# Running sums of a three-layer graph network: VectorE's loop written out, ScalarE waiting on the count of sums

## What is computed

```
def _gcn_layer(x, src, dst, norm, W, b, n_nodes):
    h = x @ W
    msg = h[src] * norm[:, None]
    out = jax.ops.segment_sum(msg, dst, num_segments=n_nodes)
    return out + b
```

## Time and profile before

| what | value |
|---|---|
| median of 3 runs (lowest, highest) | 11817.82 us (11795.35, 11846.04) |
| the profiled execution | 11829.28 us, of which the profile's span is 11827.6 us |
| busy time PE, DVE, ACT, POOL | 2554.4, 3860.8, 1826.5, 5887.5 us |
| SCALAR_TENSOR_TENSOR of the sums (line 896) | 4689, 2311.4 us busy, 493 ns each |
| indirect DMAs of the laps (line 824) | 4608, 4356.3 us busy, 945 ns each |

### The profile page before, as it was taken

How to read it: one execution, slowest core, us unless ns; L and a number is a source line. 1 busy time by engine, 2 the same in 40 slices (tenths; PEclk the granted TensorE clock), 3 DMA queues, 4 the chain that set the end, 5 groups by cost and what they waited for, 6 DMA issues and landing times. The chain is left out here.

```text
span 11827.6 us, 59944 instructions
## 1 busy us (share of the span) xinstructions
PE 2554.4 (22%) x11366; PEld 2079.0 (18%) x11366; DVE 3860.8 (33%) x7516; ACT 1826.5 (15%) x2792; POOL 5887.5 (50%) x6228
## 2 busy tenths in 40 slices
PE   6090000000040000000030000000262766655570
PEld 5070000000030000000030000000151655444460
DVE  7574333333332333333333333333340111100127
ACT  0000111111131111111131111111110111111120
POOL 0003666666636666666646666666437233344411
PEclk9999999999985555555565555555665877777785
DMA  0005555555554555555555555555441111111127
GB/s 15 9 0 162 180 180 191 179 180 186 177 168 158 182 186 180 176 183 176 180 161 174 183 183 177 182 175 191 157 140 24 36 37 37 34 34 34 34 85 223
DMA packets 586804, 1580.96 MB, mean 134 GB/s; under 512 B 134656, under 2 KB 373580, under 8 KB 547948
## 3 DMA queue, kind: packets, MB, share of 16 engines
q1 hardware_dynamic: 306828, 897.27, 21.2%
q0 software_dynamic: 278608, 668.34, 19.2%
q10 hardware_dynamic: 1296, 14.68, 0.3%
HBM read 820.05 MB, written 759.77 MB: 134 GB/s over the span
## 5 line engine op out<-in xcount | busy, mean ns | idle before, releaser
L824 POOL DMA_INDIRECT acc<-feature_table,staged_indices x4608 | 4356.3, 945 | 3043.4 <-issue 1523.7
L896 DVE SCALAR_TENSOR_TENSOR ps<-ps,keep_within_node,acc 128x256 f32<-128x256 f32 x4689 | 2311.4, 493 | 4521.2 <-issue 3756.1
L1205 POOL DMA_INDIRECT acc<-attention_table,idx x1024 | 972.6, 950 | 1312.5 <-DVEq L1422 978.1
L862 PE MATMUL ps<-work,carry_from_partition 128*128 128x256 f32 x6 | 3.7, 713 | 6986.2 <-ACT work L777 6986.2
L862 PEld LDWEIGHTS ps<-work,carry_from_partition 128*128 128x128 f32 x6 | 1.5, 309 | 6987.2 <-ACT work L777 6987.2
L777 ACT COPY acc<-ps 128x1024 f32<-128x1024 f32 x594 | 601.1, 1012 | 3249.0 <-remote 1664.4
L777 ACT COPY work<-ps 128x1024 f32<-128x1024 f32 x579 | 585.3, 1011 | 2370.9 <-remote 1006.0
L1284 PE MATMUL ps<-work 128*128 128x256 f32 x3136 | 801.8, 402 | 524.8 <-issue 451.1
L1294 PE MATMUL ps<-work,onehot 128*128 128x256 f32 x3136 | 783.2, 394 | 544.5 <-issue 501.1
L1384 DVE TENSOR_TENSOR acc<-ps,work 128x512 f32<-128x512 f32 x196 | 135.4, 691 | 2329.6 <-DMA feature_table<-acc 1057.0
L1284 PEld LDWEIGHTS ps<-work 128*128 128x128 f32 x3136 | 630.9, 202 | 681.2 <-issue 522.3
(11 more groups left out here) (308 smaller groups left out, 2226.4 us busy)
## 6 DMA issues: line engine op xcount, KB each, us to landing
unning_features_of_edges<-acc SPq DMA_DIRECT2D x147, 2048.0 KB
unning_features_of_edges<-work SPq DMA_DIRECT2D x144, 2048.0 KB
acc<-feature_table,staged_indices POOLq DMA_INDIRECT x4608
expert_rows<-acc SPq DMA_DIRECT2D x196, 256.0 KB
onehot<-feature_table SPq DMA_DIRECT2D x147, 256.0 KB
acc<-expert_rows SPq DMA_DIRECT2D x25, 1024.0 KB, 6.5
feature_table<-acc SPq DMA_DIRECT2D x98, 256.0 KB
work<-expert_rows SPq DMA_DIRECT2D x24, 1024.0 KB, 7.2
```

Source lines behind the costliest of these rows:

```text
L824: nc.gpsimd.indirect_dma_start(out=rows_in[r][:, k], out_offset=None, in_=table, in_offset=bass.IndirectOffsetOnAxis(ap=staged[:, r, k:k + ...
L896: nc.vector.scalar_tensor_tensor(state[k], state[k - 1 if k else before], keep1[:, bass.ds(c + k, 1)], rows_in[r][:, k], ALU.mult, ALU.add ...
L1205: nc.gpsimd.indirect_dma_start(out=rows[:, i % 2, c], out_offset=None, in_=gat_table, in_offset=bass.IndirectOffsetOnAxis(ap=idx[1][:, i * ...
```

## The change

DVE's laps are no loop any more: all 1,563 columns of a layer stand in the program one after another, with constant addresses and constant counts. The count of sums, now called `columns_summed`, runs through the whole layer (it was cleared in each lap). Each sum waits for the count just before itself, where before the wait stood behind the sum. The semaphore `four_summed` is gone: ACT waits for a value of `columns_summed` that stands for the same event (the first column of the next four is done; at the very end, the last column). ACT, POOL, SP and PE keep their loops and the order of their work. In `copies_of` the line `w = min(4, size - 4 * j)` moved up, since the wait needs it. The same holds for all three layers.

```
                     def copies_of(begun, r, uses, size):
                         for j in range(groups(size)):
-                            act.wait_ge(s_sum, begun + (j + 2))
+                            w = min(4, size - 4 * j)
+                            act.wait_ge(s_c, begun + (2 + 4 * j + w - (size == LAST[-1] and j == groups(size) - 1)))
...
-                            copies_of(g * 16 + r * 4, r, g, U)
+                            copies_of(g * (4 * U) + r * U, r, g, U)
...
                     nc.vector.memset(state[U - 1], 0.0).then_inc(s_c, 1)
-                    dve.wait_ge(s_c, 1)
-                    dve.sem_clear(s_c)
-
-                    def sums(m, r, uses, size, c, seen, before=U - 1):
+                    before = U - 1
+                    for m, r, uses, size, c in [(m, m % 4, m // 4, U, m * U) for m in range(4 * LAPS)] + tails:
                         dve.wait_ge(s_row[r], uses * (16 * U) + (row_base[r] + 16 * size))
                         for k in range(size):
                             if k % 4 == 0:
                                 dve.wait_ge(s_free, m * 4 + (k // 4 + 1))
+                            dve.wait_ge(s_c, c + k + 1)
                             nc.vector.scalar_tensor_tensor(
-                                state[k], state[k - 1 if k else before], keep1[:, bass.ds(c + k, 1)], rows_in[r][:, k],
+                                state[k], state[k - 1 if k else before], keep1[:, c + k:c + k + 1], rows_in[r][:, k],
                                 ALU.mult, ALU.add).then_inc(s_c, 1)
-                            dve.wait_ge(s_c, seen + k + 1)
-                            if k % 4 == 0:
-                                dve.sem_inc(s_sum, 1)
+                        dve.wait_ge(s_c, c + size + 1)
                         dve.sem_inc(s_used, 1)
-                    with dve.Fori(0, LAPS) as g:
-                        for r in range(4):
-                            sums(g * 4 + r, r, g, U, g * (4 * U) + r * U, r * U)
-                        dve.sem_clear(s_c)
...
-                    dve.sem_inc(s_sum, 1)
```

More of the change, by code:

```diff
@@ L746, in layer @@
             s_out = [sem(f"sums_out{r}" + n_) for r in range(4)]
-            s_stg, s_tick, s_c, s_sum, s_free, s_used = (sem(c + n_) for c in (
-                "indices_staged", "pool_tick", "sum_chain", "four_summed", "four_copied", "rows_used"))
+            s_stg, s_tick, s_c, s_free, s_used = (sem(c + n_) for c in (
+                "indices_staged", "pool_tick", "columns_summed", "four_copied", "rows_used"))
             s_carry, s_fixd = sem("carries" + n_), sem("fix_done" + n_)
@@ L772, in copies_of @@
                         for j in range(groups(size)):
-                            act.wait_ge(s_sum, begun + (j + 2))
+                            w = min(4, size - 4 * j)
+                            act.wait_ge(s_c, begun + (2 + 4 * j + w - (size == LAST[-1] and j == groups(size) - 1)))
                             if j == 0:
                                 act.wait_ge(s_out[r], uses * 16 + 16)
-                            w = min(4, size - 4 * j)
                             nc.scalar.copy(sums_out[r][:, 4 * j:4 * j + w].rearrange("p c f -> p (c f)"),
@@ L782, in _ @@
                         for r in range(4):
-                            copies_of(g * 16 + r * 4, r, g, U)
+                            copies_of(g * (4 * U) + r * U, r, g, U)
                             put(g * 4 + (4 + r), r)
                     for r in range(4):
-                        copies_of((LAPS - 1) * 16 + r * 4, r, LAPS - 1, U)
-                    begun = LAPS * 16
+                        copies_of((LAPS - 1) * 4 * U + r * U, r, LAPS - 1, U)
                     for m, r, uses, size, c in tails:
-                        copies_of(begun, r, uses, size)
-                        begun += groups(size)
+                        copies_of(c, r, uses, size)
                     act.sem_inc(s_zt, 4)
@@ L895, in sums @@
                                 dve.wait_ge(s_free, m * 4 + (k // 4 + 1))
+                            dve.wait_ge(s_c, c + k + 1)
                             nc.vector.scalar_tensor_tensor(
-                                state[k], state[k - 1 if k else before], keep1[:, bass.ds(c + k, 1)], rows_in[r][:, k],
+                                state[k], state[k - 1 if k else before], keep1[:, c + k:c + k + 1], rows_in[r][:, k],
                                 ALU.mult, ALU.add).then_inc(s_c, 1)
-                            dve.wait_ge(s_c, seen + k + 1)
-                            if k % 4 == 0:
-                                dve.sem_inc(s_sum, 1)
+                        dve.wait_ge(s_c, c + size + 1)
                         dve.sem_inc(s_used, 1)
-                    with dve.Fori(0, LAPS) as g:
-                        for r in range(4):
-                            sums(g * 4 + r, r, g, U, g * (4 * U) + r * U, r * U)
-                        dve.sem_clear(s_c)
-                    before, seen = U - 1, 0
-                    for m, r, uses, size, c in tails:
-                        sums(m, r, uses, size, c, seen, before)
-                        seen += size
                         before = size - 1
-                    dve.sem_inc(s_sum, 1)
                     dve.wait_ge(s_carry, 1)
```

## The result

| | before | changed |
|---|---|---|
| median of the runs | 11,827.0 us (4 runs, 11,795.4 to 11,846.0) | 11,553.7 us (4 runs, 11,545.7 to 11,567.2) |
| ratio | | 0.9773, 95% interval 0.9748 to 0.9797 |
| span of the profiled execution | 11,827.6 us | 11,543.9 us |
| first gather of a layer to its leading rows, three layers | 2275.1, 2289.6, 2285.2 us | 2192.3, 2192.3, 2191.9 us |

The changed kernel is 2.3% faster, by 273 us. 8% were forecast: 10,880 us, with a range up to 11,150. The direction was right and the size far off.

The account below looks back on a forecast made before the run. DVE was taken to set the pace, 92.0 us a lap of 64 columns against POOL's 80.0. Three sum stages of 1953.5 + 14 = 1967.5 us save 947 us from 11,829.3: 10,880 us, range 10,840 to 11,150.

Parts of the forecast that it names:

- The pauses went: Sign of being right: POOL's waits for staged indices, 74 before, remain only at the start of each layer.
- The written-out loads: Rival at DVE's queue: written-out instructions cost more than looped ones, being loaded for one use; 12,480 us, chance 0.03.
- ACT's semaphore: Part of the change: ACT waits for the same event under another name; no separate gain, its share counted in DVE's column price.
- The node stage: Sign of being right: the stage behind the first sum stage, 247.8 us, stays unchanged.
- (4): POOL's gathers in a sum stage: POOL is the next limit, issuing 1563 gathers at 1.25 us, 1953.5 us.
- (5): End of a sum stage: with DVE on time, the leading rows follow the last gather by 14 us, not 30.5.
- a busier shared port: Rival: gathers wait for the port POOL shares with DVE, 1.74 us apart; 13,180 us, chance 0.02.
- a fuller DMA: Rival: transfers become the bound, with 0.57 the most that lasts, a lap of 86 us; 11,310 us, chance 0.03.
- step (1): DVE's queue: instructions per column fall from 2.6 to 1.3, so a column costs 1.15 us and a lap 74 us.
- the slow stretch: Part of DVE's lap, 66.8 us: 30 sums start 2.3 us apart, register instructions between them at a median of 700 ns.
- The rival that DVE stays in front: DVE still sets the pace in slow stretches, at 1.8 or 2.3 us a column; 11,100 or 11,385 us, chance 0.17.
- The "issue" of rows 3: Time between POOL's gathers: 1523.7 us in 4534 pieces, read as a fixed 0.30 us behind each gather.

Follow-up runs that it names:

- mix1_again: Changed kernel with layer 1 storing 1 of 16 columns and layer 2 summing one column in four: 11,564.1 us on the slower chip; 9328.9 us on a faster one.
- mix2_again: Changed kernel, layer 1 gathering 64 of 256 features per row, layer 2 with one sum in four and 1 of 16 columns stored: 11,552.7 us, slower chip.
- extra_per_column: Changed kernel with one more DVE semaphore instruction behind each sum: 11,654.5 us on the slower chip.
- written_sum_again: Changed kernel, but ACT still waits for the semaphore that DVE counts up every four columns: 11,560.7 us on the slower chip.
- loop_act_counts: Kernel before with its loop kept, ACT waiting for a running count of sums, the wait moved before the sum: 9332.4 us on a faster chip, ratio 0.9995.
- loop_act_again: Kernel before with its loop kept, ACT waiting for a running count of sums, the wait moved before the sum: 12,025.2 us on the slower chip.
- fewer_rows: Changed kernel gathering 128, 64 and 32 rows in layers 0, 1 and 2: 9140.3 us on a faster chip.

## Why the prediction was wrong

**Right.** The pauses went: 74 waits for indices became 3. The written-out loads cost nothing. ACT's semaphore was worth nothing by itself. The node stage didn't move. On the 9,335 chips a stage takes what (4) and (5) add up to, 1966.2 us against 1967.5. But every variant takes it there, the kernel before's loop with ACT's new wait too, so it is no gain of the change.

**Wrong: step (4).** "Is the 1.25 safe with a busier DVE and more traffic? ... So I leave it." The check behind it was a stretch of 20.1 us with 16 gathers. The longest unpaused run that the trace held was this, of the attention stage (each layer begins with 111 or 112 unpaused gathers as well):

```profile
L1205 POOL DMA_INDIRECT acc<-attention_table,idx x128: 938/944/1070, 9393.8 to 9555.5; - x128
```

128 gathers in 161.7 us. The change was to make runs of 1563. The slowing sets in after about 180, so no row could show it, and a burst rate was taken for a lasting one. Gathers took 2161 us of a stage instead of 1953.5: 208 of the 225 us by which a stage missed. The forecast had called a busier shared port or a fuller DMA the ways to a longer spacing, at 1.74 us a gather and at a lap of 86 us, 1.34 a gather. The spacing did grow, to 1.38 over the loop, yet by neither mechanism: mix1_again and mix2_again took away three quarters of DVE's sums and three quarters of the rows' bytes for nothing. (The forecast tells the port rule of the Trainium skill, "SBUF — State Buffer", section "SBUF: two separate sides", without its condition: there the lock needs a DVE instruction in a 2-port mode or with two SBUF inputs. Of the sum's two tensors one, the state, lies in PSUM, so it is doubtful that the rule bears on this kernel at all.)

**Wrong: step (5).** It took DVE to be on time at the end. DVE trails by 19 columns; 30.9 us instead of 14, the other 17 us of the 225. (On the 9,335 chips, where DVE is on time, the end takes 12.6 us.)

**Wrong: step (1).** It put DVE's column at 1.15 us, under POOL's 1.25, so that POOL would set the pace. 0.88 us per queue instruction was the slow stretch divided by 2.6. Measured over whole stages it is about 0.064 us (2.3 to 3.4 per column), a fourteenth. A column of 1.3 instructions takes 1.40 us (2192.3 / 1563) and one of 2.3 takes 1.43 (2233.6 / 1563). The wait that it left out is DVE's wait for its own sum before, 0.8 us at 2909 sums, which writing out doesn't remove. Had the gathers stayed at 1.25 us, DVE's 1.40 would still have made laps of 90 us: 10,880 + 3 x 24 x 9.6 = 11,570, an estimate. The two errors don't add up, for both limits lie at 1.40. The rival that DVE stays in front had its condition met, a price over 1.25, but its prices of 1.8 and 2.3 us, its fast stretches and its sign, pauses of POOL in each lap, were wrong, and its times (11,100 to 11,385) miss as well.

**A smaller misreading.** The "issue" of rows 3 isn't a fixed 0.30 us: 1523.7 us in 4534 pieces are 0.336 each. Some 160 us of further pauses stand in it, so POOL paused more often than the 74 waits say.

How this bears on the kernel before is argued and not shown: its looped gathers, pauses included, stood 1.43 us apart in layer 0, 3% over the 1.38 of the changed kernel, and extra_per_column has pauses and 1.40. That suggests that its slow stretches and pauses were the form in which it met a limit near 1.40 us, which the changed kernel meets as longer gathers, and not 80 us of POOL plus 12 us of DVE's lateness per lap.

**Open.** What takes the 1.40 us is not settled, neither for the gathers nor for DVE's chained sums. That the gathers don't pay it per byte is shown; whether per gather or per row, and whether semaphore updates are what queues, was asked by four kernels that met only 9,335 chips. The first theory of mix1, one queue event per 0.7 us and engine and two of them to a gather, fits both rates and isn't excluded; it leaves open why 180 gathers go at 1.25 us first. Nor is it settled why DVE's columns stay near 1.4 us for 25 us after the last gather, when sums in pairs during full gathering (mix1_again, layer 2) stand 0.63 us apart. No version beats the changed kernel on the 11,830 chip: written_sum_again equals it, and the others are slower.

## What to carry to other kernels

When a change removes pauses, ask what the pauses had hidden: look for the longest stretch in the trace in which the next bound already runs without one, and if there is none as long as what the change makes, put the average with its pauses into the range. A long duration of an instruction in a slowed stretch is not its price; the price is what one more of them adds to the stage, and it can be a tenth of that. When an engine's queue gets shorter, ask also which waits of its own chain stay. Where waits against a running count are made inside a loop, count the register instructions that they need, and measure on more than one chip before a gain is called a gain of the code.

## What the runs showed of the hardware

- The same kernel took 11,785 to 11,846 us in the first measurement and on chip 14, and 9,320 to 9,349 on four others. The first gather of the sums starts at 1031 to 1032 us in both, so nothing before it differs. Of some 2,500 us, three sum stages make about 950 (2275 to 2290 us in the first measurement, 1966 in loop_act_counts), a node stage about 97 (247.8 against 150.9), and the expert stage, where gathers of the attention table run too, about 1,210 (its first to last matmul 2,559 us, against 1,349).
- On the slower chip, gathers run 1.25 us apart for about 180, then 1.40 on average, and 1536 of them span 2123 us to 0.3 us under each load tried without pauses.
- There a queue instruction of DVE can take 0.70 or 1.40 us, against 0.046 us on a faster chip (0.70 us is the median in the slow stretch of the earlier trace rows and 0.69 of the extra instruction), but not every one does: the register instructions of loop_act_again have a median of 40 ns and a maximum of 1.41 us.
- Chained sums, each waiting for the one before, stand 1.40 us apart there and 0.53 on a faster chip. They keep near the first step for 25 us after the last gather, with the transfers silent for 11 of them.
- A gather of 32 rows is hardly cheaper for POOL than one of 128: 1.17 us against 1.25 from start to start (fewer_rows, a faster chip).
